# First expert stage's routing placed inside the latent attention's steps; four VectorE operations on ScalarE, the latents turned a step later

## What is computed

```python
def mla_attention(x, ...):
    q = (x @ Wq.T)...; latent = layernorm(x @ Wdkv.T, ln_g, ln_b)
    k = (latent @ Wuk.T)...; v = (latent @ Wuv.T)...
    q = apply_rope(q); k = apply_rope(k)
    ...                               # causal softmax, 16 heads of 8
    return out @ Wo.T

def moe(x, gate_w, gate_b, W1, b1, W2, b2):
    logits = x @ gate_w.T + gate_b
    top = jnp.argmax(logits, axis=-1)
    onehot = jax.nn.one_hot(top, N_EXPERTS, dtype=x.dtype)
    h = jax.nn.relu(jnp.einsum('btd,ehd->bteh', x, W1) + b1)
    y = jnp.einsum('bteh,edh->bted', h, W2) + b2
    return jnp.einsum('bted,bte->btd', y, onehot)

x = x + _L0_xattn_ref(_layernorm(x), ctx_1024, ...)
x = x + _L0_ffn_ref(_layernorm(x), ...)       # r = r + mla(rmsnorm(r)); r + moe(rmsnorm(r))
x = x + _L1_xattn_ref(_layernorm(x), ctx_1024, ...)
x = x + _L1_ffn_ref(_layernorm(x), ...)       # 8 experts, two for each token
```

## Time and profile before

| | us |
|---|---|
| median of 3 runs | 2046.31 |
| lowest, highest | 2046.07, 2053.31 |
| the profiled execution, device time | 2049.34 |
| its span | 2047.5 |

### The profile page before, as it was taken

The page is one execution under the profiler, slowest core; times in us unless marked ns, Lnnn a source line. Parts: engine busy times, 40 slices in busy tenths (PEclk is TensorE's granted clock), DMA queues, the critical chain, the costliest instruction groups (busy, mean ns, idle before and its releaser), DMA issues. The chain is left out here.

```text
span 2047.5 us, 63292 instructions
## 1 busy us (share of the span) xinstructions
PE 1493.7 (73%) x22193; PEld 1111.0 (54%) x22194; DVE 1348.0 (66%) x3733; ACT 1172.9 (57%) x2974; POOL 773.1 (38%) x823
## 2 busy tenths in 40 slices
PE   0688888846888877788424992888888884499991
PEld 0466666624555555556223780566666663377781
DVE  4577777636777777776454664678777875366665
ACT  2366666623544444444433990798888883377770
POOL 0000000022322323231485561336666666466661
PEclk9999999967999999999556995899999996699996
DMA  7110000000001000000012223000011111222227
GB/s 231 32 34 27 31 31 25 26 6 27 31 20 33 21 29 25 26 33 18 23 43 72 74 66 96 12 12 30 29 32 32 31 36 33 79 81 77 81 77 250
DMA packets 110889, 100.81 MB, mean 49 GB/s; under 512 B 17827, under 2 KB 98598, under 8 KB 110656
## 3 DMA queue, kind: packets, MB, share of 16 engines
q1 hardware_dynamic: 87648, 67.02, 11.0%
q0 software_dynamic: 12928, 25.60, 3.8%
q10 hardware_dynamic: 10080, 5.01, 0.8%
HBM read 43.25 MB, written 32.96 MB: 37 GB/s over the span
## 5 line engine op out<-in xcount | busy, mean ns | idle before, releaser
L2497 POOL DMA_INDIRECT e_back<-e_out_rows,e_G x142 | 148.4, 1045 | 98.8 <-issue 56.7
L664 DVE TENSOR_REDUCE m_mx<-m_pM 128x8 f32<-128x1024 f32 x128 | 155.6, 1216 | 29.6 <-PE m_pM L375 29.5
L1459 ACT ACTIVATE w_weights<-w_pS,w_ng 128x77 f32<-128x77 f32 x512 | 157.8, 339 | 17.7 <-DVE w_ng L1547 17.5
L526 ACT ACTIVATE m_PT<-m_pS 128x1024 f32<-128x1024 f32 x128 | 130.4, 1019 | 59.3 <-PE m_pS L404 58.0
L1112 POOL DMA_INDIRECT e_rows<-re_R,re_index x128 | 126.1, 985 | 63.7 <-issue 35.2
L526 ACT ACTIVATE a_PT<-a_pS 77x1024 f32<-77x1024 f32 x128 | 130.5, 1019 | 17.8 <-PE a_pS L404 12.6
L2520 DVE TENSOR_TENSOR e_gl<-e_g,e_gh 128x512 f16<-128x512 f32 x142 | 98.3, 692 | 57.4 <-ACT e_g L2464 53.7
L769 POOL TENSOR_SCALAR a_var<-a_aggr 128x4 f32<-128x4 f32 x16 | 3.1, 193 | 337.0 <-DVE a_aggr L590 337.0
L1660 POOL TENSOR_TENSOR w_weights<-w_weights,w_rec 128x616 f32<-128x616 f32 x64 | 77.9, 1217 | 125.4 <-DVE w_rec L1551 125.0
L664 DVE TENSOR_REDUCE a_mx<-a_pM 128x8 f32<-128x616 f32 x128 | 101.5, 793 | 33.0 <-PE a_pM L375 33.0
L1459 ACT ACTIVATION_READ_ACCUMULATOR w_weights<-w_pS,w_ng 128x1 f32 x512 | 113.6, 222 | 0.0
(11 more groups left out here) (383 smaller groups left out, 5651.1 us busy)
## 6 DMA issues: line engine op xcount, KB each, us to landing
e_G<-e_rows SPq DMA_DIRECT2D x106, 132.0 KB, 2.3
e_B<-e_back SPq DMA_DIRECT2D x16, 512.0 KB, 6.9
stage<-in_split SPq DMA_DIRECT2D x13, 512.0 KB, 4.6
Qs<-a_qh SPq DMA_DIRECT2D x128, 32.0 KB
Qs<-m_qh SPq DMA_DIRECT2D x128, 32.0 KB
Ks<-m_kh SPq DMA_DIRECT2D x32, 128.0 KB
e_R<-e_back SPq DMA_DIRECT2D x16, 256.0 KB, 3.5
w_stage<-in_late SPq DMA_DIRECT2D x16, 256.0 KB, 2.6
```

Source lines behind the costliest of these rows:

```text
L526: act.activation(PT[:NK, b % 2, 8 * half:8 * half + 8, :], pS[:NK, :, :], ACT.Exp, scale=float(1.0 / np.sqrt(HD))).then_inc(exp_done, 1)
L664: dve.tensor_reduce(out=mx[:, 8 * half:8 * half + 8], in_=pM[:, :, :NK], op=ALU.max, axis=AX.X).then_inc(m_max, 1)
L1459: ac = act.activation(weights[:, b % 2, n, :], pS[:, n // HB, n % HB, :KC], ACT.Exp, bias=ng[:, b % 2, n:n + 1], scale=float(WD) ** -0.5, ...
L2497: pool.indirect_dma_start(out=back, out_offset=bass.IndirectOffsetOnAxis(ap=G[:, r, s, D:D + 1].bitcast(I32), axis=0), in_=out_rows[:, r, ...
```

## The change

In the latent attention a Routing object for the first expert stage (names re_... with 4 experts, in the change) and a Tables object are made. Routing of group g-1, g-2 and g-3 is placed into the steps of group g: squares (ScalarE, step 2), roots (GpSimd, step 2), shrink (ScalarE's scaled rows, step 3); turn (TensorE), hi (ScalarE) and lo (VectorE) in two halves (steps 0 and 1), score (TensorE, step 3), keep (VectorE, step 3); for a pair of groups pick (step 3 of odd groups), rank and stand (step 2 of even ones), and two or one row stores in the steps (send, GpSimd). X + Y is made by GpSimd (join, step 3). Pieces for the last groups stand in finish. mixture's own routing is gone, and experts now serves both expert stages.

Beside it: mT, the copies of V, the RMS rows and latT's two results are made by ScalarE; latT moves from slot (3,1) to (0,0) of the next group and q from (0,0) to a new slot (0,2) behind the first maxima; the latents are normalized later in step 3; the loop holds four groups; the stage frees its semaphores at its end.

```diff
         if latent:
-            order = ["q", "qs", "k", "ks", "v", "x", "lat", "latT"]
-            first_use = 3
+            order = ["latT", "q", "qs", "k", "ks", "v", "x", "lat"]
+            first_use = 2
...
-            slots = {(0, 0): "q", (0, 1): "qs", (1, 0): "k", (1, 1): "ks", (2, 0): "v", (2, 1): "x",
-                     (3, 0): "lat", (3, 1): "latT"}
+            slots = {(0, 0): "latT", (0, 2): "q", (0, 1): "qs", (1, 0): "k", (1, 1): "ks", (2, 0): "v", (2, 1): "x",
+                     (3, 0): "lat"}
...
-            groups(engine, lambda g, p, nxt, nxt2: [step(g, p, b, nxt, nxt2) for b in range(GB)])
+            groups(engine, lambda g, p, nxt, nxt2: [step(g, p, b, nxt, nxt2) for b in range(GB)], 4 if latent else 2)
...
+            def routing(g, b):
+
+                made, scored, chosen, ranked = routed(g)
+                if b < 2 and scored:
+                    route.turn(pe, scored, rows_bank, b)
+                if b == 2 and ranked:
+                    route.rank(pe, ranked, rank_bank)
+                if b == 3 and scored:
+                    route.score(pe, scored, score_bank)
...
                 if two:
                     project_output(*two)
+                routing(g, b)
                 if before:
                     values(gp, pp, bp)
...
+                if latent:
+                    keep_max(g, b)
+                if first and (first == "latT" or not latent):
+                    part(first, ga, (p + far_a) % 2)
                 if two:
                     output_hi(*two)
                 exps(g, p, b, 0)
...
                 if latent and b == 1 and nxt2:
                     squares(shift(g, 2))
...
+                if latent and b == 2 and nxt2:
+                    rms_rows(shift(g, 2))
...
+                made, scored, chosen, ranked = routed(g)
+                if b < 2 and scored:
+                    route.hi(act, scored, rows_bank, b)
+                if b == 2 and made:
+                    act.wait_ge(res_done, lin(g, GB, 0))
+                    settle(act, c)
+                    route.squares(act, made)
                 exps(g, p, b, 1)
+                if b == 3 and made:
+                    route.shrink(act, made)
...
+                if what == "lat":
+                    latents(gw)
+                made, scored, chosen, ranked = routed(g)
+                if b < 2 and scored:
+                    route.lo(dve, scored, rows_bank, b)
+                if b == 2 and ranked:
+                    route.stand(dve, ranked, rank_bank)
+                if b == 3 and scored:
+                    route.keep(dve, scored, score_bank)
+                if b == 3 and chosen:
+                    route.pick(dve, chosen, 0)
+                    route.pick(dve, chosen, 1)
                 if more:
                     take_max(gn, bn, 1)
                     negate(gn, bn)
...
+                made = routed(g)[0]
+                if b == 2 and made:
+                    route.roots(pool, made)
+                away, first, count = leaving(g, b)
+                if count:
+                    route.send(pool, away, first, count)
+                if b == 3 and made:
+                    join(made)
...
+            def finish():
+                route.send(pool, ENDING, 0, 8)
+                route.roots(pool, LAST)
+                join(LAST)
+                route.send(pool, END, 0, 8)
+                route.all_sent(pool)
...
-def mixture(nc, c, X, S, second, parts, out=None):
-
+def experts(nc, c, X, second, parts, out=None):
...
-        narrow_attention(nc, c, X, Y, True)
+        with nc.cleanup_on_exit():
+            narrow_attention(nc, c, X, Y, True)
...
-            mixture(nc, c, X, Y, False, lambda k, a, n: c["parts"].of(("w1a", "w2a")[k], a, n))
+            experts(nc, c, X, False, lambda k, a, n: c["parts"].of(("w1a", "w2a")[k], a, n))
```

More of the change, by code:

```diff
@@ L292, in walk, with routed, leaving @@
             begin()
-            groups(engine, lambda g, p, nxt, nxt2: [step(g, p, b, nxt, nxt2) for b in range(GB)])
+            groups(engine, lambda g, p, nxt, nxt2: [step(g, p, b, nxt, nxt2) for b in range(GB)], 4 if latent else 2)
             finish()
+        LAST, BEFORE = (None, NG - 1), (None, NG - 2)
+        ENDING, END = pair((None, NG - 3)), pair(LAST)
+        rows_bank, score_bank, rank_bank = pT[:, P:3 * P], pT[:, 3 * P:3 * P + 64], pT[:, 3 * P + 64:]
+        end_banks = pP[:, :2 * P], pM[:, 0:2, :].rearrange("p h x -> p (h x)")
+        def routed(g):
+            if not latent:
+                return None, None, None, None
+            made, scored, before = [None if g[0] is None and g[1] < by else shift(g, -by) for by in (1, 2, 3)]
+            odd = g[1] % 2
+            return made, scored, pair(scored) if scored and odd else None, pair(before) if before and not odd else None
+        def leaving(g, b):
+            far, first, count = ((4,) + ((2, 2), (4, 2), (6, 1), (7, 1))[b]) if g[1] % 2 else (3, 0, 2 if b == 3 else 0)
+            return (None, 0, 0) if g[0] is None and g[1] < far else (pair(shift(g, -far)), first, count)
         def hi_count(g, what):
             per = [w for w in order if w in (("x", "qs", "ks", "latT") if latent else ("x", "q", "k"))]
-            lead = 2 if latent else 1
-            back = 1 if what in ("x", "latT") else 0
+            lead = 1
+            back = 1 if what == "x" else 0
             return lin(g, len(per), lead + per.index(what) + 1 - back * len(per))
@@ L482, in finish @@
                 turn_heads(g, GB - 1)
+                if latent:
+                    pe.wait_ge(evac, use(g, "v") + 1)
+                    pe.wait_ge(m_max, 2 * NB)
+                    route.rank(pe, ENDING, rank_bank)
+                    route.turn(pe, BEFORE, end_banks[0], 0)
+                    route.turn(pe, BEFORE, end_banks[1], 1)
                 turn_output(g, GB - 1)
                 project_output(g, GB - 1)
+                if latent:
+                    pe.wait_ge(route.placed, lin2(ENDING, 1, 1))
+                    route.score(pe, BEFORE, score_bank)
+                    route.turn(pe, LAST, end_banks[0], 0)
+                    route.turn(pe, LAST, end_banks[1], 1)
+                    pe.wait_ge(route.kept, lin(BEFORE, 1, 1))
+                    route.score(pe, LAST, score_bank)
+                    pe.wait_ge(route.kept, lin(LAST, 1, 1))
+                    route.rank(pe, END, rank_bank)
             walk(pe, begin, step, finish)
@@ L558, in step @@
                 exps(g, p, b, 0)
+                if first and first != "latT" and latent:
+                    part(first, ga, (p + far_a) % 2)
                 if one:
@@ L633, in part @@
                                       ALU.mult).then_inc(evac, 1)
-                elif what == "v":
+                elif what == "v" and not latent:
                     dve.wait_ge(used, u + 1)
@@ L719, in begin @@
                 negate((None, 0), 0)
+                if latent:
+                    dve.wait_ge(route.brought, 16 * len(route.tables))
             def step(g, p, b, nxt, nxt2):
@@ L726, in step @@
                 two = earlier(g, b, 2)
-                keep_max(g, b)
+                if not latent:
+                    keep_max(g, b)
                 what, gw, far = slot(b, 0, g, nxt, nxt2)
@@ L756, in finish @@
                 divide(g, GB - 1)
+                if latent:
+                    route.stand(dve, ENDING, rank_bank)
+                    route.lo(dve, BEFORE, end_banks[0], 0)
+                    route.lo(dve, BEFORE, end_banks[1], 1)
                 output_lo(g, GB - 1)
                 residual(g, GB - 1)
+                if latent:
+                    route.keep(dve, BEFORE, score_bank)
+                    route.lo(dve, LAST, end_banks[0], 0)
+                    route.lo(dve, LAST, end_banks[1], 1)
+                    route.keep(dve, LAST, score_bank)
+                    route.pick(dve, END, 0)
+                    route.pick(dve, END, 1)
+                    route.stand(dve, END, rank_bank)
+                    tables.count(dve)
             walk(dve, begin, step, finish)
@@ L844, in _ @@
             sp.wait_ge(zeroed, 3)
+            if latent:
+                route.bring(sp)
+                tables.bring(sp)
             def begin():
@@ L853, in step, with finish @@
                     stack(sp, shift(g, 1), 1 - p, "k")
-            walk(sp, begin, step, lambda: None)
+            def finish():
+                if latent:
+                    tables.fill(sp, 0)
+            walk(sp, begin, step, finish)
 TS, SUB = 256, 2
```

656 lines of the change are left out of this document (98 added, 558 removed).

## The result

The changed kernel takes 2077.28 us against 2047.95 us of the kernel before, measured beside it: ratio 1.0136, interval 1.0102 to 1.017. The forecast was 2022, faster; the time lies outside its range. The profiled execution has a span of 2069.1 us, 21.6 more than before.

What follows compares the result with a forecast made beforehand. Bound: a dependency ring through the latent attention's steps, then a 118 us routing stage paced by GpSimd's row stores. -118.3 + 37.3 - 10.0 + 59 + 4 + 4 = -24.0, giving 2022 us; 8-in-10 range 1990 to 2056.

Steps and rivals of the forecast that it cites:

- Part 1: Behind the latent attention: the separate routing stage goes, -118.3 us, and a tail of +37.3 us comes back.
- Part 2: Latent attention's loop and start: fewer loop turns, -7.7 us, and an earlier first maximum, -2.3; -10.0 in all.
- Part 3: Latent attention's steps with routing inside: +4.9 us in each of 12 groups, from 30.93 to 35.85 us a group.
- 59 + 4 + 4: Latent attention's steps: 59 us for 12 groups, 4 for the last group, 4 for TensorE's clock.
- Step 1: Second step of a group: 10.0 us, before 6.81, as VectorE's lo waits for ScalarE's hi behind four squares.
- the wait for the stacked keys: TensorE's wait in step 3, 16.7 us in 15 groups before, was to be gone.
- Steps 2 and 3: Last two steps of a group: mean 17.2 us together, before 16.43, with mT of step 3 at 11.2 after ng.
- Four operations leave VectorE: Latent attention's steps: some 3.4 us a group moves from VectorE to ScalarE, routing work comes in; balance near nothing.
- GpSimd ... placed behind the rotation sums: GpSimd in the steps: sends, join and root fit, 20 of 36 us busy; only ll late, ready just in time.
- +4 for TensorE's clock: Latent attention's steps: TensorE idles 2.6 us in step 1, some 1.7 in step 2; its lower clock adds 4 us.
- B: Rival, latent attention's steps: gaps bring TensorE to 1.2 GHz for half the steps, some 40 us a group, 2070 us; chance 0.12.
- A: Rival, latent attention's steps: routing taken in at no cost beyond TensorE's work, 1973 us; chance 0.09.

Runs made afterwards that it cites:

- b_loop4: The kernel before with the latent attention's loop holding four groups instead of two, nothing else: ratio 0.9964, -7.3 us.
- a_four_back: The changed kernel with mT, V's copies, the RMS rows and the latents' scaled result back on VectorE, routing still inside: ratio 0.9988.
- b_moves: The changed latent attention (moves to ScalarE, new slots, four-group loop) without routing inside, the routing stage of before behind it: ratio 1.0103 to the kernel before.
- best3: best1 with all four operations (mT, the latents' scaled result, V's copies, RMS rows) back on VectorE: ratio 0.9625, 1970.58 us.
- best3_lock: best3 with GpSimd's two orders as in the changed kernel again (row root ahead of ll, join at the end of step 3): ratio 0.9749.
- b_gap: The kernel before with two more 1.21 us reductions, results unread, ahead of the second maximum of step 1: ratio 1.0222.
- e2_join_early: The changed kernel with GpSimd's join moved from the end of step 3 to step 2, ahead of the routing's roots: ratio 1.0104.
- best1: The changed kernel with five orders altered: ll and join earlier, hi ahead of squares, routing's squares to step 1's end, pick in step 0: ratio 0.9776, 1996.91 us.

## Why the prediction was wrong, by its own steps

**Part 1, the routing stage and its end: the total was right, two of its terms were not.** 37.8 us for 37.3. From the timeline of the kernel after, the root of the last group, the index, and the last send:

```profile
1099.13 1.04 POOL L1258 TENSOR_TENSOR re_rstd<-re_var,mhalf 128x4 f32<-128x4 f32 x1
...
1107.61 0.17 DVE L1248 CAST re_index<-re_slots 128x8 int32<-128x8 f32 x1
...
1117.55 0.96 POOL L1279 DMA_INDIRECT e_rows<-re_R,re_index  x1 [0.31 <-issue]
```

From the root's end to the index it is 7.6 us where the forecast took 9.8, and from the last send to the first load 10.4 where it took 7.3. The two misses nearly cancel, which is luck; why the first load comes 3 us later than at the wide attention's end stays open.

**Part 2, loop and start: right.** -7.3 measured alone for -7.7. The start's -2.8 for -2.3 is weak support: b_loop4, which leaves latT where it was, has its first ng 1.5 us earlier than before too.

**Part 3, the steps: the term was 59 + 4 + 4 and measured 116** (108.1 and the 7.7 of the loop). Its pieces:

- Step 1 was 10.0 and measured 10.09; lo's wait was 2.5 and measured 2.49. Of the wait for the stacked keys 1.1 us is left of 16.7. These rest on rows of the same chain, and held.
- Steps 2 and 3 were 17.2 and measured 19.75. mT of step 3 was to start 11.2 us after ng; it starts at 12.0 in groups 2 and 3 and at 12.9 in the mean, 14.0 where step 2's clock was 0.50. From that ol to ng it was 4.3, and 6.7 in odd groups; it is 4.1, and 7.6 in the odd groups from 5 on, where pick's comparison is held. The chain was the right one, and clock and lock lie on it.
- "Four operations leave VectorE ... a balance near nothing" failed. Between the end of ng and ol of step 0 VectorE was idle for 1.7 of 3.8 us already before (0.9 of 3.0 in b_loop4), and is for 3.9 of 4.3 after: what it gives away there shortens nothing, and ScalarE's work stands on the ring. The balance is +30 us (a_four_back), and +28 for the bundle with the slots (b_moves against b_loop4). The forecast had the passes over latT in step 0, but counted 3.35 us from the end of ng to ol, where the mean of groups 2 to 13 is 4.33.
- "GpSimd ... placed behind the rotation sums; it is 20 of 36 us busy. The one late there is ll" failed. GpSimd was priced by its own time alone. join and ll meet ng and pick on the ring: 20 us of excess in the changed kernel, and 25 us when it was put back into best3 (best3_lock). This had no term at all.
- "+4 for TensorE's clock" was mis-sized. The idle 2.6 us in step 1 was foreseen, but behind it the low stretch covers much of step 2 (all of it in two of the 12 groups), and in six groups a second one lies over part of step 0: TensorE is busy 4.3 us longer a group in the mean, 1 to 2 of them with the routing's own work. b_gap gives it a price of 0.97 us a group for a 2.27 us gap in the kernel before, 14 us in 14 groups; here some groups have two gaps, and what the clock costs in all was not measured by itself.

The three overlap, since a wait for one lets the clock fall and a low clock makes the next wait: undone one at a time (lock 8 and 7, moves 30, the wait of step 1 25, the routing's squares 11) they give 81 us and not the excess of 49. The last two of these undo waits that the forecast had in its 59.

**The rivals.** B ended nearest: it had 40 us a group and 2070, and the result is 40.2 and 2077. It had 0.12. That its group came out is luck: its mechanism was TensorE's clock low in half of the steps, with a clock under 0.8 as its sign, and the steps had 0.87; the group shown above (0.71, 0.96, 0.50, 0.86) is one of the two lowest. A, that the steps take the routing in almost for nothing, is not what this change does, but what best3 comes to, with the four operations back on VectorE: A said 1973, best3 took 1970.58.

**What could have been read in the trace of before.** The wide attention has the same pair of engines at work beside each other, and there the small operation ahead of its exponentials varies. From the timeline of the kernel before, VectorE beside GpSimd, and then the group of that operation:

```profile
1411.53 1.22 POOL L1660 TENSOR_TENSOR w_weights<-w_weights,w_rec 128x616 f32<-128x616 f32 x1
1412.21 0.59 DVE L1547 TENSOR_SCALAR w_ng<-w_mx 128x8 f32<-128x8 f32 x1
...
1417.76 0.17 DVE L1547 TENSOR_SCALAR w_ng<-w_mx 128x8 f32<-128x8 f32 x1
```

```profile
L1547 DVE TENSOR_SCALAR w_ng<-w_mx 128x8 f32<-128x8 f32 x64 | 22.8, 356 | 4.2 <-issue 2.1
```

0.59 us with GpSimd's 1.22 running to 1412.75, 0.17 when the next of these has just ended (1417.71); 356 ns in the mean. The view that groups instructions shows it at a glance: one shape, one engine, and a mean of twice the smallest.

The Trainium skill, SBUF — State Buffer, Who interferes with whom, states the rule: VectorE and GpSimd share a pair of SBUF ports that is locked for a whole instruction, and the order of issue decides who blocks; an operation of VectorE with two SBUF inputs, or a copy, cast or scalar operation in a fast two-port form, takes part, and one with at most one SBUF input outside these forms does not. The traces agree: ng, a scalar operation from SBUF to SBUF, and pick's comparison, with two SBUF inputs, were held to the end of ll and join (most of them 0.6 to 1.4 us long), the maxima out of PSUM never (1216 ns). The change puts ll (1.14 us) and join (1.28) beside the ng of steps 0 and 3, so by this rule it had a price of its own; the prediction did not weigh it.

## What to carry to other kernels

An operation moved off a busy engine can cost time where that engine was waiting anyway and the new one stands on the ring: read what the giver does in that stretch (here VectorE, idle for 1.7 us of the 3.8 ahead of ol before anything was moved) before counting its relief. When GpSimd gets work beside VectorE, look where its SBUF operations will run against the small SBUF operations that close a step, and place them beside reads of PSUM or beside waits. The same routing inside the same steps was 1.4% slower or 3.75% faster than before by order and engine alone, so price a change that fills gaps by what each gap's neighbour waits for, not by the gap.

## What the runs showed of the hardware

- A small SBUF operation on VectorE (0.17 us) lasted up to 1.34 us while one GpSimd operation worked on SBUF, and once 1.96 us, from within a row store to the end of the join behind it; join's 1.28 us beside it are no more than the 1.26 of GpSimd's sum over as many elements.
- The low-clock stretch of TensorE moves with the gaps: the same operations in the same group had 1.00 and 0.63 in steps 1 and 2, and with one GpSimd operation placed earlier 0.84 and 0.78. A gain in one step was so given back in another (e2_join_early: -0.94 and +0.8).
- A row store of 0.96 us held ng too, but only in its later part: ng begun 0.51, 0.59 and 0.70 us into one lasted 0.42, 0.35 and 0.26 us, to just short of the store's end (e2_join_early twice, after), and begun 0.33 us into one it had its 0.17 (best3).
- A gap of 2.3 us ahead of ng cost 3.2 us a group (b_gap).
- The one turn of the loop costs 2.7 us in b_loop4 (step 0 9.60 for 6.91) and 5.5 in best1 (14.8 for 9.3). TensorE's wait for issue is 2.3 and 3.4 us; the rest in best1 comes with a low clock in that step (0.65 where the other groups have 1.00). Its row among the waits of best1:

```profile
PE m_pT L428 <- issue: 3.4, 1, 3.4
```
